# Another interleaving of the first pair's projections, maxima and values, and of the assemblies' copies, in a fused expert and attention kernel

## The reference

```python
x = x + 0.5 * ffn(layernorm(x))
x = x + attn(layernorm(x))
x = x + 0.5 * ffn(layernorm(x))
```

```python
c_kv = x @ W_kv_down
k_rope = rotary(c_kv @ W_k_rope, cos, sin)
k = (c_kv @ W_k_up).reshape(B, T, 16, 8)
v = (c_kv @ W_v_up).reshape(B, T, 16, 8)
q = (x @ W_q).reshape(B, T, 16, 8)
q_rope = rotary(x @ W_q_rope, cos, sin)
scores = (q . k per head) + (q_rope . k_rope, the same for all heads)
w = softmax(where(causal, scores / sqrt(40), -inf))
attn = (w @ v) @ W_o
```

## Time and profile before

| | |
|---|---|
| median of 3 runs | 618.35 us (617.75 to 620.77) |
| profiled execution | 620.18 us, span of instructions 618.5 us |
| busy, of the span | PE 86%, DVE 70%, ACT 41%, POOL 15% |
| mean granted TensorE clock | 0.928 of 2.4 GHz |
| stage of the change | about 150 to 200 us of the span |

### The profile page before, as it was taken

The page is one execution under the profiler, slowest core; times in us unless marked ns, Lnnn a source line. Parts: engine busy times, 40 slices in busy tenths (PEclk is TensorE's granted clock), DMA queues, the critical chain, the costliest instruction groups (busy, mean ns, idle before and its releaser), DMA issues.

```text
span 618.5 us, 11436 instructions
## 1 busy us (share of the span) xinstructions
PE 529.7 (86%) x3411; PEld 336.7 (54%) x3435; DVE 431.8 (70%) x1404; ACT 253.3 (41%) x405; POOL 94.9 (15%) x208
## 2 busy tenths in 40 slices
PE   2867999867798999999999999999987636899986
PEld 1745787653373555555555555555533533577764
DVE  5875888764659476777867677767810787879874
ACT  3523122123361456564555556554576320121212
POOL 3700000001500112131221212121222150000000
PEclk9679899987798799999999999999999758899999
DMA  8694221000061000000000000000020000112102
GB/s 232 176 283 138 76 77 45 32 2 3 0 258 67 1 21 26 12 25 27 27 27 26 28 16 25 15 26 27 0 80 0 1 1 0 39 47 71 49 27 69
DMA packets 27502, 32.47 MB, mean 52 GB/s; under 512 B 7009, under 2 KB 18753, under 8 KB 27329
## 3 DMA queue, kind: packets, MB, share of 16 engines
q1 hardware_dynamic: 26784, 31.61, 16.9%
q10 hardware_dynamic: 672, 0.28, 0.2%
HBM read 21.76 MB, written 9.96 MB: 51 GB/s over the span
## 4 chain that ended last, share of the span: by engine, by line
PE 69%; DVE 18%; issue 5%; ACT 4%; DMA 2%; SPq 1%; DVEq 1%; ACTq 0%; POOL 0%
PE ps L1271 12%; PE ps L1336 11%; PE ps L1061 10%; PE ps L1309 9%; PE ps L1093 7%; PE ps L1105 5%; DVE mxh L925 3%; PE ps L1112 3%; PE ps L1002 2%; DVE summed L922 2%; PE ps L1267 2%; ACT probs L663 1%; PE ps L1211 1%; PE ps L1065 1%; PE ps L1013 1%
## 5 line engine op out<-in xcount | busy, mean ns | idle before, releaser
L663 ACT ACTIVATE probs<-ps 128x1024 f32<-128x1024 f32 (+2 forms) x192 | 148.2, 810 | 128.1 <-PE ps L1309 128.0
L925 DVE TENSOR_REDUCE mxh<-ps 128x1 f32<-128x512 f32 (+2 forms) x176 | 117.5, 690 | 50.3 <-PE ps L1271 48.3
L1271 PE MATMUL ps<-Kst,Qst 120*128 120x512 f32 (+3 forms) x384 | 137.4, 422 | 7.5 <-DVE mxh L925 4.3
L1271 PEld LDWEIGHTS ps<-Kst,Qst 120*128 120x128 f32 x384 | 68.5, 196 | 66.8 <-DVE mxh L925 23.7
L1309 PE MATMUL ps<-Qst,Kst 121*128 121x512 f32 (+3 forms) x384 | 96.3, 357 | 1.9 <-ACT probs L663 1.7
L922 DVE CUSTOM_DVE_ANT_0 summed<-ps,maskf 128x384 f32<-128x384 f32 (+1 forms) x128 | 76.2, 621 | 23.1 <-PE ps L1271 21.3
L495 POOL TENSOR_SCALAR_AFFINE_SELECT probs<-probs 128x256 f32<-128x256 f32 x128 | 52.0, 406 | 232.5 <-ACT probs L663 231.8
L1336 PE MATMUL ps<-probs,Vst 128*32 128x512 f32 (+3 forms) x768 | 82.7, 503 | 1.2 <-POOL probs L495 1.2
L1309 PEld LDWEIGHTS ps<-Qst,Kst 121*128 121x128 f32 x384 | 67.5, 192 | 22.4 <-ACT probs L663 7.3
L1061 PE MATMUL ps<-onehot,xp 128*128 128x512 bf16 (+1 forms) x245 | 68.2, 397 | 9.5 <-DVE onehot L785 8.0
L785 DVE TENSOR_SCALAR onehot<-iotab,posm 128x128 bf16<-128x128 bf16 (+1 forms) x352 | 59.2, 247 | 3.3 <-issue 2.5
(11 more groups left out here) (167 smaller groups left out, 595.1 us busy)
## 6 DMA issues: line engine op xcount, KB each, us to landing
gus<-guT_d SPq DMA_DIRECT2D x14, 384.0 KB, 3.5
wgn<-in_L_ffn_gate_up_proj SPq DMA_DIRECT2D x8, 384.0 KB, 4.9
guT_d<-gus SPq DMA_DIRECT2D x8, 384.0 KB, 4.6
dns<-dnT_d SPq DMA_DIRECT2D x14, 192.0 KB, 3.4
Kst<-kn_d SPq DMA_DIRECT2D x28, 64.0 KB
Qst<-qn_d SPq DMA_DIRECT2D x28, 64.0 KB
wdn<-in_L_ffn_down_proj SPq DMA_DIRECT2D x8, 192.0 KB, 5.5
dnT_d<-dns SPq DMA_DIRECT2D x8, 192.0 KB, 5.1
```

The lines of the kernel that those rows point to most:

```text
L663: e.activation(probs[n % RING][:, 2 * b:2 * b + 2, lo:BANK], ps[:, 2 * b:2 * b + 2, lo:BANK], ACT.Exp, scale=SCALE).then_inc(probs_ready, 1)
L925: e.tensor_reduce(to, s.rearrange("p (q k) -> p q k", k=w), AX.X, ALU.max).then_inc(mx_ready, 1)
L1271: ins = e.matmul(ps[:, bank, i * w:(i + 1) * w], Qst[p][h][0:ROWS, column(b, jt * P):column(b, jt * P) + P], Kst[p][h][0:ROWS, column(b, o ...
```

## The change

It has five parts:

- `beside`: projection u now stands behind unit 2u (units 0, 2, ... 14) instead of unit u. The rest of projection u stands behind unit 2u + 2, ahead of projection u + 1, instead of behind unit u + 2.
- `VALUES`: the four groups of values stand behind units 18, 22, 26 and 30 instead of 10 to 13.
- The copies of the assemblies: ScalarE makes 0, 1, 2, 4, 5, 8, 9, 12, 13, and VectorE 3, 6, 7, 10, 11, 14, 15. ScalarE makes copy 0 ahead of the second rope's high half.
- The banks: rounds 1 and 3 use 0, 6, 7, 2, round 2 uses 3, 4, 5, 1. Round 1 waits for copy 0, since it takes bank 2. The waits for the second side's low parts move from round 1 to round 2.
- VectorE rotates the second side ahead of its low rest, and ScalarE copies the low half of projection u - 1 ahead of the high half of projection u.

```diff
--- before.py
+++ after.py
@@ -83,11 +83,12 @@
 TH = BANK // P
 BEFORE = [sum(SHARE[:n]) for n in range(NS + 1)]
 NC = N // BANK
+VALUES = [4 * NC + 2 + 4 * g for g in range(NG)]
 NOPES = [(0, 0), (1, 0), (0, 2), (1, 2), (0, 1), (1, 1), (0, 3), (1, 3)]
 ASM = [(side, c, h) for side in range(2) for h in range(2) for c in range(N // BANK)]
-ASMBANK = ((2, 3, 4, 5), (0, 1, 6, 7))
+ASMBANK = ((2, 3, 4, 5), (0, 6, 7, 2), (3, 4, 5, 1), (0, 6, 7, 2))
 NB = 6
-BYDVE = [k for k in range(len(ASM)) if k % 2]
+BYDVE = [3] + [k for k in range(N // BANK, len(ASM)) if k % 4 >= 2]
 
 
 def asm_outs(k):
@@ -616,7 +617,7 @@
             def assembled(k):
                 side, c, h = ASM[k]
                 e.wait_ge(asm_done, k + 1)
-                e.activation((Qst, Kst)[side][0][h][0:ROWS, piece(c)], ps[0:ROWS, ASMBANK[k // NC % RING][c], :], ACT.Copy).then_inc(asm_act, 1)
+                e.activation((Qst, Kst)[side][0][h][0:ROWS, piece(c)], ps[0:ROWS, ASMBANK[k // NC][c], :], ACT.Copy).then_inc(asm_act, 1)
 
             def nope_high(u):
                 e.wait_ge(nope_done, u + 1)
@@ -631,13 +632,14 @@
             low_high(0)
             rope_high(0)
             low_high(1)
+            assembled(0)
             rope_high(1)
-            for k in range(len(ASM)):
+            for k in range(1, len(ASM)):
                 if k not in BYDVE:
                     assembled(k)
-            for u in range(2 * NC + 2):
-                if u >= 2:
-                    nope_low(u - 2)
+            for u in range(2 * NC + 1):
+                if u >= 1:
+                    nope_low(u - 1)
                 if u < 2 * NC:
                     nope_high(u)
             for g in range(NG):
@@ -900,13 +902,13 @@
             rotate(0)
             low_rest(0)
             rope_low(0)
+            rotate(1)
             low_rest(1)
-            rotate(1)
             rope_low(1)
             for k in BYDVE:
                 side, c, h = ASM[k]
                 e.wait_ge(asm_done, k + 1)
-                e.tensor_copy((Qst, Kst)[side][0][h][0:ROWS, piece(c)], ps[0:ROWS, ASMBANK[k // NC % RING][c], :]).then_inc(asm_dve, 1)
+                e.tensor_copy((Qst, Kst)[side][0][h][0:ROWS, piece(c)], ps[0:ROWS, ASMBANK[k // NC][c], :]).then_inc(asm_dve, 1)
 
             def maxima(pair, first, last, banks=RING):
                 for m in range(first, last):
@@ -1186,11 +1188,13 @@
                     e.wait_ge(hi_ready, 1)
                     e.wait_ge(lo_ready, 1)
                 elif r == 1:
+                    e.wait_ge(rsum_ready, 2)
+                    e.wait_ge(asm_act, 1)
+                elif r == 2:
                     e.wait_ge(lowl_ready, 2)
-                    e.wait_ge(rsum_ready, 2)
-                else:
                     e.wait_ge(hi_ready, 2)
                     e.wait_ge(lo_ready, 2)
+                if r >= 2:
                     by_act, by_dve = asm_outs((r - 1) * NC - 1)
                     e.wait_ge(asm_act, by_act)
                     e.wait_ge(asm_dve, by_dve)
@@ -1198,7 +1202,7 @@
                                          (spread[:, side, 0, :], rh, ROPE3), (spread[:, side, 1, :], rl, ROPE3)):
                     for c in range(NC):
                         strip = slice(c * DR, (c + 1) * DR)
-                        ins = e.matmul(ps[0:rows, ASMBANK[r % RING][c], :], table[strip, :], src[side][strip, :], start=src is lh, stop=src is rl,
+                        ins = e.matmul(ps[0:rows, ASMBANK[r][c], :], table[strip, :], src[side][strip, :], start=src is lh, stop=src is rl,
                                        skip_group_check=True)
                         if src is rl:
                             ins.then_inc(asm_done, 1)
@@ -1223,12 +1227,12 @@
 
             def beside(m):
 
-                if 2 <= m < 2 * NC + 2:
-                    rest(m - 2)
-                if m < 2 * NC:
-                    nope(m)
-                if 2 * NC + 2 <= m < 2 * NC + 2 + NG:
-                    values(m - 2 * NC - 2)
+                if m % 2 == 0 and 1 <= m // 2 <= 2 * NC:
+                    rest(m // 2 - 1)
+                if m % 2 == 0 and m // 2 < 2 * NC:
+                    nope(m // 2)
+                if m in VALUES:
+                    values(VALUES.index(m))
 
             e.wait_ge(xnT_ready, 2 * NG + RING)
             e.wait_ge(ckvT_ready, NC)

```

## The result

The changed kernel takes 616.74 us (median of 20 runs, 610.93 to 620.03), and the kernel before 619.52 us (20 runs, 616.51 to 621.81). The ratio is 0.9949, with a 95% interval of 0.9930 to 0.9967: some 3 us faster (2.8 between the medians), where 3.7 had been forecast from the 618.35 us of three runs. The profiled executions differ less, 618.48 against 620.18 us.

A forecast was written before the change was run, and what follows sets the result against it. The stretch before the attention steps was bound by TensorE, then VectorE, both paid in sum. Gains of 2.8 us up to the join and 0.8 behind it, from the 618.35 us median, gave 614.6 us; own range 612.5 to 616.5.

The forecast's parts named there:

- The sum: Whole kernel: 2.8 us gained up to the join plus 0.8 behind it, 3.6 us in all.
- rival B: Gain lost in SP's queue or in ScalarE waits longer than 0.45 us; 617 us, chance 0.18.
- Piece 1: Assembling Q and K: round 2 starts 1.3 us earlier, first unit at 165.1 instead of 166.96, about 1.9 us gained.
- The clock through the units: From the assemblies into the units: clock falls near 160.9 and stays low until 171.05, projection 1 ending about 171.6.
- rival A: Clock stays high through assemblies and units; 7.2 us gained, 611.1 us, chance 0.25.
- Piece 2: Units with projections and values beside them: period 2.0 us for two units, projection 7 ending at 183.6.
- naive 1.55: Units: period in us for two units, a rest and a projection if the rest had no exposed wait.
- The pause ahead of a rest: Units: TensorE idle about 0.4 us before each rest, waiting for ScalarE's copy.
- Piece 3: VectorE tail of the maxima: 13.4 us without a gap from unit 15, maxima ending at 197.5 against 200.06.
- Piece 4: Clock in the first pair step: fall comes later relative to the step, +0.8 us taken, bounds -1.5 to +3.3.
- Rival C: Clock stays at half through the units, period 3.05 us, maxima 4.3 us later; 622.6 us, chance 0.05.
- the signs named beforehand: Round 2 near 160.4, first unit 164.1 to 165.2, 2.0 us period, gapless VectorE, unwaited values, SP's cover under 1.5 us.

The follow-up runs named there:

- e11: Changed kernel with rests one unit later, idle matmuls in assemblies and tail, and POOL's copies held until VectorE's second rope low part; 607.9 us, ratio 0.9836 to before.
- e1: Changed kernel with only the assemblies' part kept, units, rests and values ordered as before; 617.1 us, ratio 0.9996 to before.
- e2: Kernel before with only the units' part of the change (projections, rests, values, ScalarE's order), old assemblies; 619.5 us, ratio 1.0017 to before.
- e3: Changed kernel with each rest one unit later, behind unit 2u + 3, ScalarE's order to match; 613.5 us, ratio 0.9914 to before.
- e4: Changed kernel with the four groups of values in a row behind units 18 to 21; 618.0 us, ratio 0.9997 to before.
- e5: Changed kernel with idle matmuls behind units 31 to 37 and six ahead of the second turn of the maxima; 613.6 us, ratio 0.9896 to before.
- e8: Kernel before with idle matmuls behind units 14 to 37 and six ahead of the second turn; 617.4 us, ratio 0.9954 to before.
- e6: Changed kernel with idle matmuls in the assemblies' pauses, ahead of rounds 1 and 2 and the first unit; 613.8 us, ratio 0.9900 to before.

## Why the prediction was right

The sum, 3.6 us, came out at 2.8 in the medians and at 1.9 in the profiled executions. That it came out this near is in part luck, since terms missed in both directions. The 616.7 us measured lie just above the forecast's own 612.5 to 616.5 and next to rival B's 617, though nothing of B happened; part of that is the kernel before itself, 618.35 us by three runs and 619.52 by twenty. The terms, from the first rope matmul:

- **Piece 1** was put at 1.9 and gave 0.9 us. The sum of the rotation came when worked out. Two things were missing. The prediction cost POOL's copies at nothing, since the copies that they wait for "come no later than before". They come earlier: ScalarE's copy 0 now stands ahead of the second high half, so POOL starts at 158.22 instead of 160.21 and runs beside VectorE's low part, which takes 1.02 instead of 0.69 us (e11 shows it). And round 2, which starts at 160.68 with the clock falling at 160.7, had nothing left of the half microsecond at the high level. The late start costs 0.5 us and the low level another 0.5.
- **The clock through the units** was the wrong half of the forecast's case. It fell where it was expected, but came back at 164.1 instead of 171.05. The truth lay between the forecast and rival A, which said that it would not fall: the assemblies went as forecast and the units as in A. This gave the 2 us at the join that made up for piece 1, which was luck. e1 has it, e2 does not. The working has one slip that does no harm: the 0.86 us for units 1 and 2 is for each of them, and its 171.6 counts it twice.
- **Piece 2** was right: period 2.0 forecast, 2.04 measured. The naive 1.55 is nearly what e3 reaches (1.57) once the rest stands one unit further from its projection, for 3.3 us at the join. The pause ahead of a rest was 0.2 to 0.3 us, not 0.4.
- **Piece 3** was right: 13.4 us forecast, 13.45 measured, and e4 gives 1.8 of the 2 us that the spread values were to save.
- **Piece 4** was mis-sized: +0.8 forecast, -0.2 measured. That the low clock costs 3.1 to 3.3 us there is shown by e5 and e8. The fall came later relative to the step, as forecast, and so did the return, which the prediction did not count.
- **Not in the sum** is what came after: 0.8 us over the later pair steps and 1.0 behind the last join. In the table "end" runs from 167.3 to 170.7 us for identical work. Over the whole of it the mean clock is 0.91 before and 0.89 after, 0.92 in e11 with the shortest end and 0.87 in e5 with one of the longest. That the clock there makes the difference fits these rows, but no run took it apart.
- **Rival B** (SP's queue) did not come: 2 us were left, not 1, since the last store ended at 184.57, where 186.5 had been estimated, while the second shift left at 196.92 instead of 197.9. **Rival C** did not come either: with a pause of 0.2 to 0.3 us in most of the periods, the granted clock stayed at 1.00 from 166 to 194 us. So the swing between two levels that the Trainium skill tells of in "TensorE: Matmul & The Clock Gate", section on psum-queue depth-cycling, did not show in this trace.

Of the signs named beforehand, the period, VectorE without a gap from unit 15 and the values without a wait came. Round 2 was 0.5 us and the first unit 0.9 us later than forecast (160.86 and 166.04 in before's count), the latter outside its range, and 2.0 us, not under 1.5, were left ahead of the second shift.

One thing stays open. The timed runs of e1 and e2 show no gain (0.9996 and 1.0017), while both parts together show 0.9949 and 0.9980. In the profiled executions the parts add at the join, and at the last instruction e1 has all of the gain. The interval of e1 lies clear of the first of the two ratios and overlaps the second. Where the clock's low stretches fall in the timed runs is not recorded, only their mean, so I can't say why.

## What to carry to other kernels

When an engine waits for another's copy of its own result, what shows is the copy plus the latency of the lone instruction behind it, less the work placed between. So put enough independent work between a producer and its dependent follower: here one unit more was worth 3.3 us at the join. Ask what an engine's pauses do to its clock before tuning the order of its work: here a dozen idle matmuls in pauses gave at least as much as the reordering. And spread side work where the other engine is the limit, not where it is near.

## What the runs showed of the hardware

- Matmuls of zeros whose result nobody reads, 0.22 us each, kept the granted clock at 1.00 through pauses where it had fallen to 0.50 (e5, e6, e8). Where they fitted into the pause no cost showed: the join moved by 0.2 us or less in e5 and e8 (45.5 and 49.6, against 45.5 and 49.4).
- The low stretches stood at the same place of the program, within 0.3 us, in the two profiled executions of the changed kernel, and the first fall 9.8 to 10.1 us after the first rope matmul in nine executions of eight kernels, while timed runs of one program range over 9 us with the mean clock between 0.924 and 0.952.
- A VectorE operation with both inputs and its output in SBUF took 1.02 instead of 0.69 us beside POOL's copy of SBUF data, and one of POOL's copies 0.97 instead of 0.61. VectorE's copies out of PSUM beside the same POOL copies kept their 0.62.
